# A two-layer transformer kernel on one core: order of scores and exponentials in a step of layer 0's attention, and the steps at which empty slots are filled

## The reference

```
h = layernorm(x) * (1 + ca) + sa
q, k, v = proj(h); q, k = rope(q, k)
scores = einsum('bhqd,bhkd->bhqk', q, k) / sqrt(16)
attn = softmax(scores)
x = x + ga * ((attn @ v) @ wo.T + bo)
```

## Time and profile before

| | |
|---|---|
| time, median of 3 runs | 1436.55 us (1436.17 to 1439.98) |
| the profiled execution's own time, its span | 1440.54 us, 1439.2 us |
| mean granted TensorE clock | 0.939 of full speed |
| steps of layer 0's attention with row scores (0 to 127) | 47.45 to 304.1 us |
| end of layer 0's attention (last residual) | 344.9 us |

### The profile page before, as it was taken

One profiled execution on the slowest core, in us unless ns is written; L12 is line 12 of the kernel. 1 busy time (PEld: TensorE's weight loads), 2 busy tenths in 40 slices (PEclk: granted clock), 3 DMA queues, 4 the chain that ended last, 5 costly groups with the idle time before them and its releaser, 6 DMA issues.

```text
span 1439.2 us, 22581 instructions
## 1 busy us (share of the span) xinstructions
PE 1291.0 (90%) x6461; PEld 908.8 (63%) x6461; DVE 869.9 (60%) x2637; ACT 784.2 (54%) x1919; POOL 459.3 (32%) x589
## 2 busy tenths in 40 slices
PE   6689799887979998799999999999999977899994
PEld 5334344334556776577877777787877755577773
DVE  5678677754553355665567567766676745333555
ACT  3367575654431545676666666665666633156552
POOL 6344435220344744300010015001500150355553
PEclk9689889978989999899999999999999997999997
DMA  7652617003213553134200001000100019355764
GB/s 232 147 111 76 155 31 152 2 2 141 112 52 92 162 166 103 41 132 146 77 1 1 16 4 56 1 16 1 55 6 15 1 60 382 137 144 154 209 197 136
DMA packets 79207, 133.99 MB, mean 93 GB/s; under 512 B 13788, under 2 KB 52708, under 8 KB 77420
## 3 DMA queue, kind: packets, MB, share of 16 engines
q1 hardware_dynamic: 62128, 92.39, 20.6%
q0 software_dynamic: 15712, 38.25, 9.4%
q10 hardware_dynamic: 1248, 1.90, 0.4%
HBM read 77.20 MB, written 60.00 MB: 95 GB/s over the span
## 4 chain that ended last, share of the span: by engine, by line
PE 61%; DVE 13%; issue 8%; DMA 6%; ACT 5%; POOL 5%; another core or an unknown queue 1%; SPq 0%; DVEq 0%; POOLq 0%; ACTq 0%
PE psum L126 8%; PE psum L128 7%; PE psum L127 7%; PE psum L2007 7%; PE psum L2657 6%; PE psum L2703 4%; PE psum L1978 3%; PE psum L854 3%; PE psum L2530 3%; PE psum L883 3%; POOL results L2726 2%; PE psum L2564 2%; DVE psum L1942 2%; PE psum L778 1%; PE psum L2626 1%
## 5 line engine op out<-in xcount | busy, mean ns | idle before, releaser
L790 DVE TENSOR_REDUCE a_nmax<-psum 128x2 f32<-128x1024 f32 x128 | 155.1, 1217 | 65.3 <-PE psum L778 64.3
L869 ACT ACTIVATE a_et<-psum 128x512 f32<-128x512 f32 x256 | 139.0, 594 | 93.1 <-PE psum L854 89.7
L1953 ACT ACTIVATE a_spare<-psum,a_nmax 128x128 f32<-128x128 f32 (+3 forms) x256 | 134.9, 527 | 90.5 <-DVE a_nmax L1942 79.1
L2726 POOL DMA_INDIRECT results<-r_fin,r_to x134 | 135.9, 1015 | 126.9 <-ACT r_fin L2718 58.5
L2007 PE MATMUL psum<-a_et,a_v 128*128 128x512 f32 (+3 forms) x512 | 169.9, 434 | 1.8 <-DVE a_ctx L2024 1.6
L1942 DVE CUSTOM_DVE_ANT_0 psum<-psum,a_spare 128x128 f32<-128x128 f32 (+3 forms) x256 | 127.1, 497 | 62.3 <-PE psum L128 53.7
L2657 PE MATMUL psum<-m_w,m_xT 128*128 x536 | 150.4, 403 | 0.0
L1987 ACT ACTIVATE a_et<-psum 128x128 f32<-128x128 f32 (+3 forms) x256 | 111.5, 436 | 45.6 <-PE psum L1978 41.7
L126 PE MATMUL psum<-a_kT,a_q 128*128 128x128 f32 (+3 forms) x256 | 118.5, 463 | 5.9 <-DVE a_q L1881 5.2
L854 PE MATMUL psum<-a_stk 50*128 50x512 f32 x256 | 109.2, 503 | 15.5 <-ACT a_et L869 12.5
L1978 PE MATMUL psum<-ident,a_spare 128*128 128x128 f32 x640 | 113.1, 275 | 1.6 <-DVE a_spare L1966 1.5
(11 more groups left out here) (329 smaller groups left out, 3016.4 us busy)
## 6 DMA issues: line engine op xcount, KB each, us to landing
r_xs<-slots SPq DMA_DIRECT2D x134, 129.0 KB
slots<-empty SPq DMA_DIRECT2D x12, 1290.0 KB, 6.1
m_w<-in_experts SPq DMA_DIRECT2D x16, 768.0 KB
stacks<-a_qk SPq DMA_DIRECT2D x32, 256.0 KB, 3.8
a_stk<-stacks POOLq DMA_DIRECT2D x32, 256.0 KB, 6.8
r_shared_hid<-results SPq DMA_DIRECT2D x12, 512.0 KB
m_w<-in_experts SPq DMA_DIRECT2D x4, 1216.0 KB
a_stk<-stacks POOLq DMA_DIRECT2D x32, 128.0 KB, 6.4
```

The source lines that it names most:

```text
L790: dve.tensor_reduce(nmax[:, G % 2, qt, 2 * p:2 * p + 2], psum[:, n:n + 2, :], AX.X, ALU.max, negate=True).then_inc(s_max.sem, 1)
L869: act.activation(et[:, n % NET, 2 * p + hh, :], psum[:, 4 + hh, :], ACT.Exp).then_inc(s_e.sem, 1)
L1953: act.activation(e[:, u % NE, 0:W], psum[:, n, 0:W], ACT.Exp, bias=nmax[:, u % NE, :], scale=-1.0, accum_out=rsum[:, u % NE, :]).then_inc( ...
L2726: pool.indirect_dma_start(results[:, :], bass.IndirectOffsetOnAxis(ap=to[:, i % NI, 0:1].bitcast(U32), axis=0), ys[:, o, :], None, bounds_ ...
```

## The change

On TensorE, a step had the order T0, S, T1, PV, other matmuls; now it has S, PV, other matmuls, T0, T1. On ScalarE, the exponentials of a step came first and now come last, behind the row of maxima, the context and the work for the next batch. The fills are issued in steps 101, 109, 117 and 125.

```
+        FILL_AT = PER_BATCH * (B - 1) + 5
...
         def tensor(s):
-            for G, r in groups(s, EXP_AT, 8):
-                tensor_turned(G, r, 0)
             for G, r in groups(s, 0, 8):
                 tensor_scores(G, r)
-            for G, r in groups(s, EXP_AT, 8):
-                tensor_turned(G, r, 1)
             for G, kt in groups(s, PV_AT, TT, 2):
                 tensor_pv(G, kt)
...
+            for G, r in groups(s, EXP_AT, 8):
+                tensor_turned(G, r, 0)
+                tensor_turned(G, r, 1)
...
         def scalar(s):
-            for G, r in groups(s, EXP_AT, 8):
-                scalar_exp(G, r, 0)
-                scalar_exp(G, r, 1)
             for G, r in groups(s, NT_AT + 1):
                 scalar_nrow(G)
...
             for b, half in ahead(s, tuple(d + 1 for d in V_AT)):
                 scalar_v(b, half)
+            for G, r in groups(s, EXP_AT, 8):
+                scalar_exp(G, r, 0)
+                scalar_exp(G, r, 1)
...
         def sync(s):
...
-            j, rest = divmod(s - 12, 24)
+            j, rest = divmod(s - FILL_AT, 8)
             if rest == 0 and 0 <= j < len(k.fills) and k.fills[j][0] == 0:
                 fill_slots(k, j, s_done[s])
```

## The result

The changed kernel takes 1429.58 us (median of 11 runs, 1425.35 to 1433.3) against 1436.7 beside it (11 runs, 1429.81 to 1447.77): a ratio of 0.995 with a 95% interval of 0.9926 to 0.9974. That is 7.1 us faster, where 7.7 was forecast. Measured again beside an experiment, the ratio was 0.9898 (0.9858 to 0.9937). The profiled execution took 1430.43 us, its span is 1429.1.

What follows compares the result with a forecast made beforehand. The prediction took layer 0's attention to be paced by exponentials in quiet steps, TensorE in others, one load stall and the lower clock behind it. Terms -6.8 - 3.9 + 5.0 - 2.2 + 0.2 = -7.7 us gave 1429 us, range 1417 to 1441.

Steps and rivals of the forecast that it cites:

- The stall: TensorE's wait in step 64 for the `stk` load, delayed by step 60's fill; moving the fill gives -6.8 us.
- The clock behind it: Steps 64 to 69, run mostly at 1.2 GHz after the stall, shorten to the mean of two twins: -3.9 us.
- Quiet pairs: Step pairs with little other work, paced by exponentials: S behind late T1 costs 0.24 us, 21 times, +5.0 us.
- maxima: T0's four waits for the small DMA of maxima go, as ScalarE copies the row of maxima sooner: -2.2 us.
- ScalarE's order: ScalarE's other work now precedes a step's exponentials, but cyclically the order is unchanged: 0.
- The places of the fills: Fills issued five steps ahead of the small DMA of maxima land before it and cost nothing: 0.
- The end: At the last step, 140, PV comes ahead of T0 instead of under the exponentials: +0.2 us.

Runs made afterwards that it cites:

- e1: Kernel before with only the new places of the fills, old order inside a step: 1431.74 us against 1435.88, ratio 0.9958.
- e3: Kernel before with only the fill of step 60 moved, to step 101: 1433.55 us against 1435.88, ratio 0.9986.
- e2: Changed kernel with the fills left at steps 12, 36, 60 and 84, so the new order alone: 1441.76 us against 1435.88, ratio 1.0033.
- e8: Kernel before with new places of the fills and TensorE's step as T0, T1, S, S, PV: 1430.89 us against 1437.0, ratio 0.9962.
- e6: Kernel before with new places of the fills and only TensorE in the new order, ScalarE in the old: 1466.84 us against 1437.0, ratio 1.0209.
- e7: Kernel before with new places of the fills and only ScalarE in the new order, TensorE in the old: 1458.87 us, ratio 1.0155.
- e4: Changed kernel with ScalarE's exponentials first in step 13 alone, last from step 14 on: 1427.91 us against 1435.88, ratio 0.9951.
- e9: Kernel before with fills in steps 98, 106, 114 and 122, where the small DMA of maxima is issued: 1455.72 us against 1445.65, ratio 1.0059.
- e5: Kernel before with new places of the fills and ScalarE's copy of maxima ahead of the exponentials: 1426.1 us against 1437.0, ratio 0.9918.
- e11: Kernel before with new fill places and ScalarE's copy of maxima ahead of exponentials, measured again: 1436.86 us against 1445.65, ratio 0.9929.
- e12: Changed kernel with exponentials first in step 13, and turned scores and exponentials first from step 128 on: 1427.14 us against 1436.48, ratio 0.9926.

## Why the prediction was right

The mechanism of the two large terms, stall and clock, is shown. That the sum of all terms came so near is in part luck: the terms of the order were too large, one term was left out, and the errors partly cancel.

**The stall**, -6.8: measured -7.07 (8.96 to 1.89). That the fill made it is shown: it goes with the fill (e1, e3) and comes back with it (e2).

**The clock behind it**, -3.9: measured -4.72. Steps 64 to 69 take 10.44 us, the time of the better twin in the earlier trace rows (10.53), not the mean of both.

**Quiet pairs**, +5.0, and **maxima**, -2.2: in steps 20 to 63, 70 to 102 and 102 to 127 the profiles have +0.81, +0.75 and -0.31, in all +1.3 for these two terms' +2.8. No wait for maxima is left, so -2.2 holds, and +5.0 was too large, in its count and in its price. Behind step 20, sixteen pairs are quiet in both profiles, not 21, and they grew by 3.2 us in all, most of them by 0.16 to 0.22. So the 21 idle times that were counted do not stand for 21 such pairs. The mechanism of the pairs holds (T1 to PV 0.67), and e8 has 3.39 to the digit. In the changed kernel T0 follows T0 by 1.18 instead of 1.25, since exp0 begins 0.53 after T0 and not 0.59, so a pair costs 0.18, not 0.24. Why exp0 is sooner I have not tested.

**ScalarE's order**, 0: this step failed at one place. In the steady steps it holds, and e6 and e7 show how much hung on both engines being moved together: 2 and 1.5% for either alone. But "cyclically the order is unchanged" leaves out where the cycle begins. In step 13 no earlier exponentials exist, and the first ones came to stand behind a copy that waits for VectorE: +1.7 us, which e4 gives back.

**The places of the fills**, 0: holds, with 1.6 us for the small DMAs behind them; issued three steps sooner, in the maxima's own steps, they cost 1% (e9).

**The end**, +0.2: too small to see beside the clock.

By these stages the change is worth -7.07 - 4.72 + 1.3 + 1.7 = -8.8 us, forecast -7.7, measured 7.1 on the medians; the errors of the terms partly cancel. The two profiles differ by 10.1 (1439.2 and 1429.1), the remainder being steps 0 to 12, the end, and -4.7 behind the attention. In the first two of these the clock differs between executions of one kernel. The third is no gain that can be given to the change: what lies behind the attention takes 1089.6 and 1096.9 us in the two profiles of the changed kernel, and 1088.4 to 1098.1 over all fourteen.

Whether the two halves of the change add is not settled. The fills alone give 0.42%, the order alone costs 0.33%, both give 0.5% and 1.0% in two measurements, with intervals of 0.2 to 0.4% on each. In steps 20 to 127 of the profiles they nearly add: -9.2 us for the fills, -1.9 for the order, -10.5 for both. One thing the sum didn't have is that without the stall the old order pays 5.6 us for late maxima, not 2.2, which the new order doesn't. It isn't settled whether any version here beats the changed kernel; e5, e11, e4 and e12 lie within its intervals.

## What to carry to other kernels

A large transfer with no deadline can cost more than its own time when it is issued beside one that has a deadline: look for the issue of each in the same microseconds, and move the one that can wait; then look again, since the work that was held back now meets other transfers. When work is moved to the end of a step on one engine, move what depends on it by the same amount on the other, and check the first step of the loop by itself. An engine with idle time isn't free to be moved: GpSimd's context work, sooner by one copy on ScalarE, began beside VectorE's, and TensorE waited 1.8 us (e11). Steps of one loop, compared start to start in the trace at one granted clock, show differences of 0.2 us that whole runs bury under 5.

## What the runs showed of the hardware

Matmuls on different halves of the array's rows pass each other. In step 40 of the kernel before, the row-score matmul that starts 0.01 us after T0 is the one that signals the semaphore, that of hh = 1, which the code issues second; that of hh = 0 starts 0.33 us later, with T1. So T0, S, S, T1 takes as long as T0, T1, S, S (0.68 and 0.66 us to the next), against 0.43 for two. This contradicts the strict order of starts that the Trainium skill states ("TensorE: Matmul & The Clock Gate", The mechanism).

A 16 KB set of small DMAs that lands in 1.6 us alone took 5.6 to 6.5 beside a fill of 1290 KB in step 98 of e9, where loads of `stk` were in flight as well (e1, with the loads alone, has 2.5 to 3.1), and 3.7 to 5.0 beside each of the other three fills.

The clock stays down after the idle time is over. TensorE's clock was granted at 1.2 GHz instead of 2.4 from 168.2 us, inside the stall of the kernel before, to 188.7, 14 us behind its end, with TensorE busy throughout. In e9 it was at 1.2 GHz for 48 us from 243.2 on, inside a wait of 3.5 us, and the only further waits over 0.5 us in that time were of 0.7 and 1.0.
